# A two-layer transformer on one core: one transposing transfer per token tile, sums over later tokens in ScalarE's copy, elu's minimum on POOL, and a new timetable for layer 1

## The chip, the core and the metric

The kernel runs on one core of one Trainium2 chip. The metric is the device time of one execution in microseconds. The core's engines each run their own instruction stream in order and meet at semaphores: TensorE (PE; its weight loads are PEld), VectorE (DVE), ScalarE (ACT), GpSimd (POOL) and SyncE (SP), which here only issues transfers.

## What is computed

The input x is 16 batches of 512 tokens with 128 features, fp32. Cut to what matters here:

```python
xn = layernorm(x)
# layer 0: attention, 16 heads of 8, a bias within 64 tokens, causal
probs = softmax(q @ k.T * scale + bias)             # rope on q and k
out = relu(probs + tau / row) @ v                   # tau/row is added to masked tokens too
x = x + out @ Wo.T + fp4_ffn(xn)                    # weights, input and hidden go through fp4 blocks of 16
xn = layernorm(x)
# layer 1: linear attention, elu(.)+1 on q and k, running sums over tokens
kv, ks = cumsum(k x v), cumsum(k)
out = (q @ kv) / max(q . ks, 1e-6)
x = x + out @ w_out + moe(xn)                       # router over 4 experts, 2 chosen, and a shared expert
```

## The kernel before

A batch is four token tiles (T = 4) of 128 tokens. All work is laid out by hand on a grid of **slots**: a frame has 64 slots, and frame f computes in each slot s a piece of attention of batch f and, beside it, pieces of batches f-2 to f+1. A piece's place p counts from the start of its batch: p = 0 to 63 (the frame before the batch's attention) holds norm, projections, rope, the stacking of q and k and the fp4 gate; ATT + s lies beside its own attention; L1 + s is layer 1, one frame later; L1 + 64 and above reaches into the frame after that. Each engine walks over the same slots in the same order, so within an engine the order is fixed: first what belongs to the attention (scores, biased scores, exponentials), then the pieces of `EXTRAS` (which use the two PSUM banks of the scores), then the rest. The places stand in the table at lines 58 to 80.

**Attention of layer 0.** In each even slot TensorE makes two heads' scores (`scores`, L1122) into two banks that take turns; VectorE adds the bias and finds the maximum (`biased`, L584, `s_taken`); ScalarE takes the exponential with its sum (L954); VectorE inverts the four sums after every fourth slot (`row_rcp_of`, L591); POOL scales a slot later (`scale_probs`, L851); two to three slots on TensorE turns the blocks of 128 keys (`turn_probs`, L1132), ScalarE stores them with relu (`store_probs`, L963), and TensorE multiplies with v (`pv`, L1146).

**The turn banks.** Every transpose on TensorE takes a ticket q (`turn_ticket`, L1085) and bank 2 + q % 2, and waits until the bank's last content is stored (`t_taken`). ScalarE stores them in the order of the tickets. `intra` (L1247) also takes a turn ticket. In a slot with s % 4 == 0 up to two blocks are turned, in s % 4 == 2 the others. The `INTRA` pieces in even slots are made by TensorE ahead of the blocks, and stored by ScalarE at the slot's end (`beside`, L1019), which works as long as such a slot turns at most one block.

**Sums over later tokens.** A masked token still gets tau/row, so the output needs sums of v over the tokens of later tiles. TensorE takes the sums of xn over later tiles (`fx`, L1156, three matmuls of 3 columns, two fp32 passes each), VectorE copies them (`x_future`, L599), then `fv` (L1160) and `fy` (L1165) at slots 61 and 63 take them through Wv and Wo.

**Stacks.** q and k are split into fp16 high and low parts: ScalarE casts (L944, L945), POOL subtracts (L843, L844), and SyncE turns them by transposing transfers from `qx` and `kx` to `qkT0` (layer 0, two halves of the heads, 8 transfers of 256 columns each, in slot 33 and in the batch's own slot 1, `turn_stack0`, L410) and `qkT1` (layer 1, two transfers of 512 columns per tile in slots 28 to 31, `turn_stack1`, L422). `qkT0` has one buffer, so a half is turned when the earlier batch's scores of that half are done.

**Layer 1.** Projections in slots 20 to 23 (L1111), rope on VectorE (L557 to L564) and its addition on POOL (L836), elu: minimum on VectorE (`elu_low`, L647, three buffers), exponential on ScalarE (L981), maximum and sum on VectorE (`elu_high`, L651). Then `kv` (L1170), the turn of q (`q32`), the masked products `lin` (L1179 on TensorE, L616 on VectorE, pairs in odd slots from 35), `intra` (L1253), the totals `tot` (L1189, L1191). Between them the 15 gate and up matmuls of the experts (L1203, L1213; ScalarE's tanh L977, VectorE's L633 and L640), each expert's down matmuls in four quarters (`down1`, L1268), and VectorE's accumulation (`accumulate`, L708), four slots after an expert's first quarter. The router's 16 small VectorE steps stand two to a slot from slot 31 on, after a pair in slot 28.

Of the kernel before, what the change touches and what calls it, by code (L numbers as in the profile page):

```python
# [162 lines left out]
def build(nc, x, wq, wk, wv, wo, bias, tau, tau_col_in, wg, wu, wd, wqkv1, wout1, eg, eu, ed,  # L163
          cos, sin, ident, tri, inv_row, inv_col, head_mask, head_of, suffix, sel, lower, out):
# [3 lines left out]
    with ExitStack() as ctx:  # L168
# [230 lines left out]
        def _(sp):  # L399
# [10 lines left out]
            def turn_stack0(b, half):  # L410

                sp.wait_ge(lo_ok[0].sem, lo_ok[0].at(b, 2 * T))
                if has(b - 1):
                    sp.wait_ge(s_ps.sem, plan.score["score", b - 1, (half + 1) * SLOTS // 2 - 1] + 1)
                groups = slice(half * G // 2, (half + 1) * G // 2)
                heads = slice(half * H // 2, (half + 1) * H // 2)
                for t in range(T):
# [54 lines left out]
        def _(dve):  # L472
# [170 lines left out]
            def elu_low(b, t):  # L643
                dve.wait_ge(qk_ok[1].sem, qk_ok[1].at(b, t + 1))
                if t >= 3:
                    dve.wait_ge(elu_ok.sem, elu_ok.at(b, t - 2))
# [750 lines left out]
```

## Time and profile before

| | |
|---|---|
| runs | 2138.5, 2142.2, 2140.8 us; median 2140.8 |
| profiled execution | 2139.74 us, its span 2137.9 us |
| busy share of the span | TensorE 91%, VectorE 72%, ScalarE 64%, GpSimd 54% |
| TensorE weight loads | 59% |
| mean granted TensorE clock | 0.975 |
| chain that ended last | TensorE 53%, ScalarE 15%, VectorE 12%, POOL 7%, issue 7%, SyncE's queue 3% |

Busy shares are means over the whole span; the first frame and the last have less beside each other. In the timeline a row can hold several instructions (xN) and runs from the first one's start; a note in brackets is the engine's idle time ahead of it and what ended that. A wait is put down to the releaser that came last. Matmul ends are modelled, and a fp32 matmul is two passes, hence two instructions.

### The profile page before, as it was taken

The numbers are of one execution on the slowest core, as the hardware profiler recorded it, in microseconds if no ns is written. First come the engines' busy times: TensorE is split into PE (matmuls) and PEld (weight loads), VectorE is DVE, ScalarE is ACT, GpSimd is POOL, SyncE is SP. The second block draws the span as 40 slices with busy tenths as digits, with TensorE's granted clock in tenths as the row PEclk, the third lists the DMA queues.
The fourth block names the chain that finished last, engine by engine and source line by source line (L and its number), as shares of the span: only waits on it lengthen the run. The fifth ranks groups of instructions, "written<-read, shape, count | busy, mean of one in ns | idle before, by whom it ended". The sixth has DMA issues, their size and how long they took to land.

```text
span 2137.9 us, 50103 instructions
## 1 busy us (share of the span) xinstructions
PE 1939.8 (91%) x17353; PEld 1267.2 (59%) x17353; DVE 1544.0 (72%) x5224; ACT 1376.8 (64%) x3861; POOL 1148.3 (54%) x1800
## 2 busy tenths in 40 slices
PE   3788999999999998999999899999999999998968
PEld 1455665656566574656657566565656657565646
DVE  7557778687776868777686777868777676866745
ACT  1777585676857667585766758576685856757531
POOL 4685374745637465473746547374563746555220
PEclk7779999999999999999999999999999999999989
DMA  5011011110101111010111201111010111101010
GB/s 140 18 22 33 4 29 32 28 34 19 35 10 28 33 29 32 12 38 15 29 33 28 33 4 32 28 29 34 23 33 9 28 33 24 33 12 35 4 31 6
DMA packets 180848, 59.44 MB, mean 28 GB/s; under 512 B 147835, under 2 KB 178163, under 8 KB 180595
## 3 DMA queue, kind: packets, MB, share of 16 engines
q1 hardware_dynamic: 180595, 56.23, 12.3%
q8 instruction: 139, 2.28, 0.4%
q14 instruction: 114, 0.93, 0.1%
HBM read 14.22 MB, written 4.19 MB: 9 GB/s over the span
## 4 chain that ended last, share of the span: by engine, by line
PE 53%; ACT 15%; DVE 12%; POOL 7%; issue 7%; SPq 3%; DMA 2%; ACTq 0%; DVEq 0%; POOLq 0%
PE ps L1132 10%; PE ps L1268 8%; PE ps L1203 7%; PE ps L1213 6%; PE ps L1146 5%; ACT ring L954 5%; PE ps L1122 4%; ACT pb L963 3%; SPq L428 3%; PE ps L1253 3%; DVE ring L584 3%; PE ps L1191 2%; DVE lin L616 2%; PE ps L1111 2%; DMA qkT<-kx 2%
## 5 line engine op out<-in xcount | busy, mean ns | idle before, releaser
L851 POOL TENSOR_SCALAR ring<-ring,row_rcp,tau_row 128x128 f32<-128x128 f32 (+3 forms) x1024 | 629.6, 623 | 700.8 <-DVE row_rcp L591 700.8
L954 ACT ACTIVATE ring<-ring,neg_max 128x128 f32<-128x128 f32 (+3 forms) x1024 | 570.7, 558 | 504.0 <-DVE neg_max L584 499.5
L1132 PE MATMUL ps<-identf,ring 128*128 128x128 f32 x2560 | 378.7, 287 | 9.9 <-POOL ring L851 7.6
L963 ACT ACTIVATE pb<-ps 128x512 f32<-128x512 f32 x640 | 348.6, 584 | 29.6 <-PE ps L1132 25.5
L1132 PEld LDWEIGHTS ps<-identf,ring 128*128 128x128 f32 x2560 | 279.4, 143 | 83.2 <-issue 40.1
L584 DVE CUSTOM_DVE_ANT_1 ring<-ps,bias_t 128x384 f32<-128x384 f32 (+1 forms) x496 | 286.9, 614 | 55.0 <-PE ps L1122 47.8
L1268 PEld LDWEIGHTS ps<-ed_t,h 128*128 128x128 f32 (+1 forms) x1920 | 256.5, 192 | 98.3 <-issue 94.8
L1268 PE MATMUL ps<-ed_t,h 128*128 128x128 f32 (+1 forms) x1920 | 272.7, 278 | 0.0
L1203 PE MATMUL ps<-xn1T,eg_t 128*128 128x512 f32 (+1 forms) x480 | 256.6, 616 | 2.1 <-DVE h L633 2.1
L1213 PE MATMUL ps<-xn1T,eu_t 128*128 128x512 f32 (+1 forms) x480 | 256.6, 616 | 1.1 <-DVE h L640 0.9
L616 DVE TENSOR_TENSOR lin<-ps,tri_t 128x512 f32<-128x512 f32 x256 | 164.7, 685 | 127.8 <-PE ps L1179 127.8
L977 ACT ACTIVATE tanh_t<-ps 128x512 f32<-128x512 f32 (+2 forms) x304 | 172.0, 566 | 129.5 <-PE ps L1203 125.9
L1122 PE MATMUL ps<-qkT 32*128 32x128 f16 (+3 forms) x1024 | 200.5, 309 | 47.6 <-DVE neg_max L584 23.2
L1122 PEld LDWEIGHTS ps<-qkT 32*128 32x128 f16 x1024 | 62.1, 91 | 291.3 <-issue 110.6
L584 DVE CUSTOM_DVE_ANT_0 ring<-ps,bias_t 128x128 f32<-128x128 f32 (+1 forms) x528 | 171.8, 360 | 59.1 <-PE ps L1122 58.9
L1146 PE MATMUL ps<-pb,vx 128*32 128x128 f32 x5120 | 197.8, 281 | 1.8 <-ACT o_stack L969 1.6
L954 ACT ACTIVATION_READ_ACCUMULATOR ring<-ring,neg_max 128x1 f32 x1024 | 195.3, 191 | 0.0
L633 DVE SCALAR_TENSOR_TENSOR h<-tanh_t,ps 128x512 f32<-128x512 f32 (+1 forms) x240 | 163.2, 680 | 16.5 <-ACT tanh_t L977 16.4
L640 DVE SCALAR_TENSOR_TENSOR h<-h,ps 128x512 f32<-128x512 f32 (+1 forms) x240 | 163.1, 679 | 4.9 <-PE ps L1213 3.9
L1146 PEld LDWEIGHTS ps<-pb,vx 128*32 128x32 f32 x5120 | 125.9, 111 | 42.1 <-issue 24.6
L826 POOL TENSOR_TENSOR hid<-hid,q_step 128x352 f32<-128x352 f32 x128 | 100.8, 789 | 35.7 <-DVE q_step L725 35.7
L836 POOL TENSOR_TENSOR qk<-prod 128x256 f32<-128x256 f32 x128 | 92.7, 729 | 49.2 <-DVE prod L560 48.2
(154 smaller groups left out, 2822.0 us busy)
## 6 DMA issues: line engine op xcount, KB each, us to landing
x_t<-x SPq DMA_DIRECT2D x16, 256.0 KB, 3.1
x<-x SPq DMA_DIRECT2D x16, 256.0 KB, 2.9
o_rows<-o_stack SPq DMA_DIRECT2D x256, 16.0 KB
out<-x SPq DMA_DIRECT2D x16, 256.0 KB, 2.8
qkT<-qx SPq DMA_TRANSPOSE x192, 2.4
qkT<-kx SPq DMA_TRANSPOSE x192, 2.4
bias_t<-bias SPq DMA_DIRECT2D x1, 1536.0 KB, 8.0
eg_t<-eg SPq DMA_DIRECT2D x1, 860.0 KB
```

Of the source, the lines that this page charges most:

```text
L584: dve.tensor_tensor_reduce(out=dst, in0=src, in1=add, scale=-1.0, scalar=NO_MIN, op0=ALU.add, op1=ALU.min, accum_out=neg_max[:, n % 2, r:r ...
L616: dve.tensor_tensor(lin[:, k % NLIN, :, :], src.rearrange("p (t n) -> p t n", n=P), tri_t[:, :].unsqueeze(1).broadcast_to([P, T, P]), ALU. ...
L851: pool.tensor_scalar(e, e, row_rcp[:, m % 2, r:r + 1], tau_row[:, i, HG * g + r:HG * g + r + 1], ALU.mult, ALU.add).then_inc(p_ok.sem, 1)
L954: act.activation(e, e, ACT.Exp, bias=neg_max[:, n % 2, r:r + 1], scale=-1.0, accum_out=row_sum[:, n % 2, r:r + 1]).then_inc(exp_ok.sem, 1)
L963: act.activation(pb[:, c % NPB, :], bank(turn_bank(q)), ACT.Relu).then_inc(t_taken[q % 2].sem, 1)
L977: act.activation(tanh_t[0:rows, k % 2, 0:n], bank(G0)[0:rows, 0:n], ACT.Tanh, scale=0.5).then_inc(tanh_ok.sem, 1)
L1122: pe.matmul(o[:, 0:(i + 1) * P], qkT0[rows, g, 0, i * P:(i + 1) * P], qkT0[rows, g, 1, 0:(i + 1) * P], start=True, stop=True).then_inc(s_p ...
L1132: last = pe.transpose(o[:, r * P:(r + 1) * P], ring_of(i, r)[:, k * P:(k + 1) * P], idf)
L1146: last = pe.matmul(bank(PV)[R * r:R * (r + 1), i * P:(i + 1) * P], vx0[:, b % 2, k, v0:v0 + R], pb[:, c % NPB, r * P:(r + 1) * P], start=( ...
L1203: last = pe.matmul(bank(G0)[0:n, :], eg_t[:, e, r0:r0 + n], xn1T[:, :], start=True, stop=True)
L1213: last = pe.matmul(bank(G1)[0:n, :], eu_t[:, e, r0:r0 + n], xn1T[:, :], start=True, stop=True)
L1268: last = pe.matmul(o, h1[0:n, e % 2, c, ts], ed_t[0:n, e, c, :], start=(c == 0 and e < E), stop=(c == 2))
```

## The change

- `qx` and `kx` become one tensor `qkx`; each token tile is turned by one transfer of 1024 columns, four per batch and layer. `qkT0` has two buffers. Layer 0's transfers stand in slots 12 to 15, a slot after POOL's low parts; layer 1's stay in slots 28 to 31.
- `fx`, its constant and its VectorE copy go. ScalarE's copy of the turned x becomes a plain copy of tile 0 and three Identity activations whose sums give the tiles' column sums; POOL adds them up in slot 6 (`SUM_X`). `fv` and `fy` move from slots 61 and 63 to slots 1 and 3 of the next frame.
- elu's minimum moves from VectorE (slots 22 to 25) to POOL, right behind each tile's rope addition (slots 22 and 24), with four buffers.
- Layer 1's timetable: `kv` from slots 29, 29, 31 to 33, 47, 53; the turn of q from 30 to 46; the router from 31 to 37 (its last step in slot 43); `intra` from 40, 42, 46, 53 to 40, 44, 48, 52; down quarters of experts 1 and 2 from 42 and 48 to 44 and 49; accumulations of experts 0 to 2 from slots 39, 46, 52 to 43, 48, 53.
- ScalarE stores an `intra` of an even slot right behind that slot's first exponential, ahead of the blocks.

```diff
-TURN_X, FUTURE_X, QKV0, TURN_XQ = 5, 5, 7, 10
+TURN_X, QKV0, TURN_XQ = 5, 7, 10
...
-TURN_H, FUTURE_V, FUTURE_Y = (ATT + 11, ATT + 13, ATT + 13, ATT + 15), ATT + 61, ATT + 63
+TURN_H, FUTURE_V, FUTURE_Y = (ATT + 11, ATT + 13, ATT + 13, ATT + 15), ATT + 65, ATT + 67
...
-KV, TURN_Q32 = (L1 + 29, L1 + 29, L1 + 31), L1 + 30
+KV, TURN_Q32 = (L1 + 33, L1 + 47, L1 + 53), L1 + 46
...
-INTRA = (L1 + 40, L1 + 42, L1 + 46, L1 + 53)
+INTRA = (L1 + 40, L1 + 44, L1 + 48, L1 + 52)
...
-ROUTER = L1 + 31
+ROUTER = L1 + 37
...
-DOWN1 = [GATE1[3 * e + 2] + 4 for e in range(NE - 1)] + [L1 + 65]
+DOWN1 = [L1 + p for p in (35, 44, 49, 56, 65)]
+ADD_EXPERT = [L1 + p for p in (43, 48, 53, 60, 69)]
...
+SUM_X = TURN_X + 1
+TURN_STACK0, TURN_STACK1 = QKV0 + 5, QKV1 + 8
...
-        qx = [sb(f"qx{k}", [P, T, H, R], F16) for k in range(2)]
-        kx = [sb(f"kx{k}", [P, T, H, R], F16) for k in range(2)]
+        qkx = [sb(f"qkx{k}", [P, T, 2, H, R], F16) for k in range(2)]
...
-        qkT0 = sb("qkT0", [P, G, 2, L], F16)
-        qkT1 = sb("qkT1", [P, G, 2, L], F16)
+        qkT0 = sb("qkT0", [P, 2, 2, G, L], F16)
+        qkT1 = sb("qkT1", [P, 2, G, L], F16)
...
+            def turn_stack0(b, t):
+
+                sp.wait_ge(lo_ok[0].sem, lo_ok[0].at(b, 2 * t + 2))
+                if t == 0 and has(b - 2):
+                    sp.wait_ge(s_ps.sem, plan.score["score", b - 2, SLOTS - 1] + 1)
+                sp.dma_start_transpose(qkT0[:, b % 2, :, :, t * P:(t + 1) * P].rearrange("p a g n -> p (a g) n"),
+                                       qkx[0][:, t, :, :, :].rearrange("p a h r -> p (a h r)")).then_inc(st0_ok.sem, 16)
...
-                for a, v in enumerate((qx[1], kx[1])):
-                    sp.dma_start_transpose(qkT1[:, :, a, t * P:(t + 1) * P],
-                                           v[:, t, :, :].rearrange("p h r -> p (h r)")).then_inc(st1_ok.sem, 16)
+                sp.dma_start_transpose(qkT1[:, :, :, t * P:(t + 1) * P].rearrange("p a g n -> p (a g) n"),
+                                       qkx[1][:, t, :, :, :].rearrange("p a h r -> p (a h r)")).then_inc(st1_ok.sem, 16)
...
-                    if p in TURN_STACK0:
-                        turn_stack0(b, TURN_STACK0.index(p))
+                    if 0 <= p - TURN_STACK0 < T:
+                        turn_stack0(b, p - TURN_STACK0)
...
-                    if p == DOWN1[e] + 4:
+                    if p == ADD_EXPERT[e]:
                         accumulate(b, e)
...
+            def elu_low(b, t):
+                pool.wait_ge(qk_ok[1].sem, qk_ok[1].at(b, t + 1))
+                pool.tensor_scalar(elu_m[:, t, :], qk[:, t, :], 0.0, None, ALU.min).then_inc(elum_ok.sem, 1)
...
+                if p == SUM_X:
+                    v = x_future[:, b % 2, :]
+                    pool.wait_ge(t_taken[plan.turn["x", b, 0] % 2].sem, plan.turn["x", b, 0] // 2 + 1)
+                    pool.tensor_tensor(v[:, 1:2], v[:, 1:2], v[:, 2:3], ALU.add).then_inc(xs_ok.sem, 1)
+                    pool.wait_ge(xs_ok.sem, xs_ok.at(b, 1))
+                    pool.tensor_tensor(v[:, 0:1], v[:, 0:1], v[:, 1:2], ALU.add).then_inc(xs_ok.sem, T - 2)
...
                     if p == QKV1 + ROPE1[t] + 1:
                         rope_add(b, 1, t)
+                        elu_low(b, t)
...
-                    turned(("x", b, 0), xnT[:, :])
+                    q = plan.turn["x", b, 0]
+                    act.wait_ge(t_ps.sem, q + 1)
+                    if has(b - 2):
+                        act.wait_ge(s_ps.sem, plan.score["fv", b - 2, 0] + 1)
+                    act.copy(xnT[:, 0:P], bank(turn_bank(q))[:, 0:P])
+                    for t in range(1, T):
+                        ts = slice(t * P, (t + 1) * P)
+                        ins = act.activation(xnT[:, ts], bank(turn_bank(q))[:, ts], ACT.Identity, accum_out=x_future[:, b % 2, t - 1:t])
+                    ins.then_inc(t_taken[q % 2].sem, 1)
...
-                if p in INTRA:
-                    g = INTRA.index(p)
-                    turned(("intra", b, g), nd[:, g, :])
+                if p in INTRA and p % 2:
+                    store_intra(b, INTRA.index(p))
...
                 if has(f) and s % 2 == 0:
                     exp_with_sum(f, s)
+                for b, p in plan.beside(f, s):
+                    if p in INTRA and p % 2 == 0:
+                        store_intra(b, INTRA.index(p))
                 for blk in plan.blocks(f, s):
                     store_probs(*blk)
...
-                if s % (SLOTS // 2) == 0:
-                    pe.wait_ge(st0_ok[2 * s // SLOTS].sem, st0_ok[2 * s // SLOTS].at(b + 1, 0))
+                if s == 0:
+                    pe.wait_ge(st0_ok.sem, st0_ok.at(b + 1, 0))
...
-                if name == "fx":
-                    pe.wait_ge(xn_ok[0].sem, xn_ok[0].at(b, T))
+                if name == "fv":
                     o = score_ticket((name, b, k))
-                    for j in range(1, T):
-                        last = pe.matmul(o[:, 0:T - 1], xn[:, j, :], suffix_t[:, j, :], start=(j == 1), stop=(j == T - 1))
-                elif name == "fv":
-                    o = score_ticket((name, b, k))
-                    pe.wait_ge(s_taken.sem, plan.score["fx", b, 0] + 1)
+                    pe.wait_ge(xs_ok.sem, xs_ok.at(b, T - 1))
                     last = pe.matmul(o[:, 0:T - 1], wqkv0_t[:, 2 * D:3 * D], x_future[:, b % 2, :], start=True, stop=True)
```

## Rows read from the trace of the kernel before

**Rows 1.** Stretches: length, busy us (count) by engine, clock, DMA share, GB/s.

```profile
640.70:767.10 126.40, 119.15 (x1091) 78.40 (x1091) 95.30 (x327) 85.67 (x241) 71.34 (x112) 1.00 0.12 27
...
686.00:704.67 18.67, 16.20 (x118) 8.04 (x116) 17.30 (x66) 17.81 (x53) 12.36 (x24) 1.00 0.17 33
704.67:767.40 62.73, 60.91 (x597) 40.17 (x597) 48.61 (x146) 34.08 (x92) 23.35 (x36) 1.00 0.10 21
```

**Rows 2.** TensorE's waits, four frames from 893.6 us (total, times, longest).

```profile
PE ps L1179 <- DMA qkT<-kx: 6.6, 4, 1.8
...
PE ps L1165 <- DVE neg_max L584: 3.2, 4, 0.8
```

**Rows 3.** Timeline, slots 23 to 32: start, duration, engine, line, operation, wait.

```profile
689.14 0.29 DVE L647 TENSOR_SCALAR elu_m<-qk 128x256 f32<-128x256 f32 x1
...
691.57 0.56 POOL L851 TENSOR_SCALAR ring<-ring,row_rcp,tau_row 128x256 f32<-128x256 f32 x1 [1.82 <-DVE row_rcp L591]
...
698.01 0.72 ACT L954 ACTIVATE ring<-ring,neg_max 128x512 f32<-128x512 f32 x1
...
701.01 0.69 DVE L633 SCALAR_TENSOR_TENSOR h<-tanh_t,ps 128x512 f32<-128x512 f32 x1 [0.31 <-ACT tanh_t L977]
...
701.66 0.43 POOL L843 TENSOR_TENSOR qx<-qk,qx 128x128 f16<-128x128 f32 x1 [1.11 <-ACT kx L945]
...
702.46 0.48 PE L1170 MATMUL ps<-vx,qk 128*128 128x144 f32 x2 [1.32 <-DVE neg_max L584]
...
704.67 1.09 PE L1132 MATMUL ps<-identf,ring 128*128 128x128 f32 x8
```

**Rows 4.** Timeline, slots 63 to 6.

```profile
647.63 0.83 PE L1165 MATMUL ps<-wo_t,v_future 128*16 128x128 f32 x6 [0.79 <-DVE neg_max L584]
...
653.72 0.19 ACT L954 ACTIVATION_READ_ACCUMULATOR ring<-ring,neg_max 128x1 f32 x1
...
653.81 1.64 ACT L986 ACTIVATE xn<-x_t,shift,rstd 128x128 f32<-128x128 f32 x4
...
655.48 0.69 DVE L476 TENSOR_REDUCE x_step<-xn 128x32 f32<-128x512 f32 x1 [1.36 <-ACT xn L986]
...
657.32 0.80 PE L1156 MATMUL ps<-suffix_t,xn 128*128 128x3 f32 x6
...
658.43 0.63 PE L1099 MATMUL ps<-identf,xn 128*128 128x128 f32 x4 [0.31 <-ACT pb L963]
...
659.16 0.58 ACT L920 COPY xnT<-ps 128x512 f32<-128x512 f32 x1
```

**Rows 5.** Transposing transfers: lines 419 and 428, ns min/median/max.

```profile
L419 SPq DMA_TRANSPOSE qkT<-qx x128: 1167/1247/2427, 35.9 to 1922.6; - x128
...
DMA to landing us min/median/max: 2.3/2.4/4.8
...
L428 SPq DMA_TRANSPOSE qkT<-qx x64: 1188/1264/1998, 191.1 to 2078.2; - x64
...
DMA to landing us min/median/max: 2.4/2.5/5.0
```

**Rows 6.** Timeline, slots 39 to 44.

```profile
722.48 1.09 DVE L708 SCALAR_TENSOR_TENSOR x<-ps,comb,x 128x128 f32<-128x128 f32 x4
...
730.55 0.41 PE L1179 MATMUL ps<-qkT 32*128 32x128 f16 x8
...
733.03 0.69 DVE L584 CUSTOM_DVE_ANT_1 ring<-ps,bias_t 128x512 f32<-128x512 f32 x1
...
735.84 0.41 PE L1179 MATMUL ps<-qkT 32*128 32x128 f16 x8
```

**Rows 7.** Timeline, head and tail of the program.

```profile
47.47 0.29 PE L1122 MATMUL ps<-qkT 32*128 32x128 f16 x2 [7.79 <-DMA qkT<-kx]
...
53.05 0.28 DVE L584 CUSTOM_DVE_ANT_0 ring<-ps,bias_t 128x128 f32<-128x128 f32 x1
...
2082.07 0.62 PE L1179 MATMUL ps<-qkT 32*128 32x128 f16 x8 [4.96 <-DMA qkT<-kx]
```

More of the change, by code:

```diff
@@ L79 @@
          ("q32", (TURN_Q32,)), ("intra", INTRA), ("o1", (TURN_O1,)))
-EXTRAS = (("fx", (FUTURE_X,)), ("fv", (FUTURE_V,)), ("fy", (FUTURE_Y,)), ("kv", KV), ("lin", LIN), ("tot", TOT))
+EXTRAS = (("fv", (FUTURE_V,)), ("fy", (FUTURE_Y,)), ("kv", KV), ("lin", LIN), ("tot", TOT))
 def at(table, p):
@@ L163, in build @@
 def build(nc, x, wq, wk, wv, wo, bias, tau, tau_col_in, wg, wu, wd, wqkv1, wout1, eg, eu, ed,
-          cos, sin, ident, tri, inv_row, inv_col, head_mask, head_of, suffix, sel, lower, out):
+          cos, sin, ident, tri, inv_row, inv_col, head_mask, head_of, sel, lower, out):
     NB = x.shape[0]
@@ L244, in build @@
         nd = sb("nd", [P, G, L])
-        elu_m = sb("elu_m", [P, 3, 2 * D])
+        elu_m = sb("elu_m", [P, T, 2 * D])
         qT32 = sb("qT32", [P, L])
@@ L312, in build @@
         lo_ok = two("stack_low", 2 * T)
-        st0_ok = two("stack0_turned", 16 * 2 * T)
-        st1_ok = signal("stack1_turned", 16 * 2 * T)
+        st0_ok = signal("stack0_turned", 16 * T)
+        st1_ok = signal("stack1_turned", 16 * T)
         glog_ok = signal("router_logits_stored", T)
@@ L318, in build @@
         elu_ok = signal("elu_ready", T)
+        xs_ok = signal("x_future_ready", T - 1)
         s_ps = signal("scores_in_psum")
@@ L408, in store @@
                 sp.dma_start(out[bass.ds(b, 1)].rearrange("b (t p) d -> p (b t) d", p=P), x1[:, :, :]).then_inc(y_out.sem, 16)
[L410 to L417, printed above, removed]
-                    for a, v in enumerate((qx[0], kx[0])):
-                        sp.dma_start_transpose(qkT0[:, groups, a, t * P:(t + 1) * P],
-                                               v[:, t, heads, :].rearrange("p h r -> p (h r)")).then_inc(st0_ok[half].sem, 16)
+            def turn_stack0(b, t):
[4 more added lines that the diff above has]
+                                       qkx[0][:, t, :, :, :].rearrange("p a h r -> p (a h r)")).then_inc(st0_ok.sem, 16)
             def turn_stack1(b, t):
@@ L641, in hidden @@
                                          op0=ALU.mult, op1=ALU.mult).then_inc(g_taken[1].sem, 1)
[L643 to L646, printed above, removed]
-                dve.tensor_scalar(elu_m[:, t % 3, :], qk[:, t, :], 0.0, None, ALU.min).then_inc(elum_ok.sem, 1)
             def elu_high(b, t):
                 dve.wait_ge(elue_ok.sem, elue_ok.at(b, t + 1))
-                dve.scalar_tensor_tensor(out=qk[:, t, :], in0=qk[:, t, :], scalar=0.0, in1=elu_m[:, t % 3, :],
+                dve.scalar_tensor_tensor(out=qk[:, t, :], in0=qk[:, t, :], scalar=0.0, in1=elu_m[:, t, :],
                                          op0=ALU.max, op1=ALU.add).then_inc(elu_ok.sem, 1)
@@ L1178, in into_scores @@
                         ts = slice(t * P, (t + 1) * P)
-                        last = pe.matmul(o[:, ts], qkT1[rows, g, 1, ts], qkT1[rows, g, 0, ts], start=True, stop=True)
+                        last = pe.matmul(o[:, ts], qkT1[rows, 1, g, ts], qkT1[rows, 0, g, ts], start=True, stop=True)
                 else:
@@ L1349, in shape_constants @@
         head_mask[HD * h:HD * (h + 1), h, :] = 1
-    suffix = np.zeros((P, T, T - 1), f)
-    for j in range(T):
-        suffix[:, j, 0:j] = 1
     sel = np.zeros((P, HG, NV), f)
@@ L1362, in shape_constants @@
         "inv_row": np.broadcast_to(f(1) / (pos + 1), (P, L)), "inv_col": (f(1) / (pos + 1)).reshape(T, P).T,
-        "head_mask": head_mask, "head_of": head_of, "suffix": suffix, "sel": sel, "lower": lower,
+        "head_mask": head_mask, "head_of": head_of, "sel": sel, "lower": lower,
     }
```

34 lines of the change are left out of this document (14 added, 20 removed).

## The prediction, made before the change was run

> **What bounds the kernel now.** The first view is the page's busy times by engine: TensorE works 91% of the span, VectorE 72%, ScalarE 64%, GpSimd 54%. The second is the table of stretches. A frame (64 slots; batch f's attention beside layer 1 of f-1 and the projections of f+1) lasts 126.4 us, TensorE is busy for 119 of them [rows 1], and fifteen frames, f = 1 to 15, hold layer 1 beside attention. Third, the list of waits says where the missing 7 us go: over four frames 6.6 us for the transposing transfers ahead of the first `lin` and 3.2 us at `fy` [rows 2]; the timeline adds 1.32 us a frame at the third `kv` [rows 3]. The timeline of one frame also tells which stretch is bound by what. From slot 36 to the frame's end TensorE hardly waits: what is put there is paid for. In slots 20 to 32 it waits for a chain over the other engines [rows 1, 3]: ScalarE is busy 17.8 of 18.7 us. The same edit therefore has a different price in each stretch.
>
> **What the change does to a steady frame, stretch by stretch.** Times are those of the frame that starts near 641 us. X is the start of slot 43's `lin` on TensorE.
>
> *Slots 61 to 6.* `fy` leaves slot 63, where it waited 0.79 us for the scores' bank and took 0.8; `fv` (0.24) leaves slot 61. They come back in slots 1 and 3. FX (six passes, 0.80 us) goes. But slot 5 is not held by FX: the turn of x waited until 658.43 for ScalarE's store of a probability block, which was late because VectorE's slot 4 stood behind the quantiser's reduction, which waited for ScalarE's norm [rows 4]. Replaying this chain without `fv` and `fy` in slots 61 to 63 (VectorE 0.2 us earlier, row reciprocals 0.2, POOL's rstd and the norm 0.7) brings the turn of x to about 657.65, 0.8 us earlier. Then ScalarE's copy of 0.58 us [rows 4] becomes one copy of 128 columns and three Identity passes with a sum. No row has that form. The norm's four passes of 128 columns take 1.64, and a read of the accumulator is 0.19 by itself [rows 4]. From below: the four passes with a cheaper first one, 1.3; from above: 1.64 and three reads, 2.2. I take 1.5, near the norm's passes, whose shape is the same and beside which a read can run. That is 0.9 more, and the second block of slot 6 needs this bank: it starts at 660.05 instead of 659.79. Net **+0.3 us** (-0.8 if the copy's length did not count, +0.9 at the upper end). POOL's two sums of one column (0.2 us each) wait in slot 6 behind the same copy and push the quantiser's addition by 0.3 us; its result has 2 us to spare.
>
> *Slots 20 to 32.* POOL takes four minima. VectorE's cost 0.29 each; POOL's nearest row is its scaling of 256 columns, 0.56 [rows 3]; bounds 0.29 and 0.8. Two of them delay the scaling of slots 25 to 27 by 1.1 us, so the blocks of slot 28 start some 0.3 us later, although the scores ahead of them come 0.85 us earlier (VectorE freed). Both `kv` groups of slot 29, the turn of q and the `kv` of slot 31 go. TensorE then waits for what it does not make itself: the gate of slot 31 needs slot 28's silu (701.01 + 0.6), and slot 32's blocks need POOL's fourth scaling, which stands behind the low halves of tile 2, which stand behind ScalarE's casts at 701.5; ScalarE runs almost without a gap (17.8 of 18.7 us, rows 1) up to and behind the exponential at 698.01 [rows 3]. None of these is lightened but by 0.15 us. So slot 32's transposes still start at about 704.5: **-0.15 us**, and the wait at `kv` comes back as two others.
>
> *Slot 35.* Eight transposing transfers of 1.26 us are issued one after another; the last lands 2.5 us after its issue, which is when `lin` starts [rows 5]. The waits give 6.6/4 = 1.65 us a frame. After the change four are issued, the last after POOL's last low half (about 703.9), and land by 707.2, ahead of TensorE's 709.2: **-1.65 us**. From 256 to 512 columns a transfer's issue grew from 1.247 to 1.264 us and its landing from 2.4 to 2.5 [rows 5]; now it has 1024. I take 1.3 and 2.8. The upper bound is proportional, 2.53 us each, the same ten microseconds in all: then nothing is gained here. The Trainium skill speaks for that bound: its page DMA: Bandwidth & Descriptors (section Why a DMA increments its semaphore by 16 and not by 1) has a transpose inside SBUF, on the generations before the newest, pay one push command for every tile; by that the four would take as long as the eight, and the sum would be 30 us more. The rows of 256 and 512 columns do not agree with a price per tile.
>
> *Work that moves into the full stretch.* Three `kv` at 0.3 us and the turn of q at 0.6 now stand in slots 33, 46, 47 and 53: **+1.5 us**.
>
> *Slots 42 to 45.* This is the large term. Before, `intra` 1 was in slot 42, experts' down quarters in 42 to 45, the first accumulation in slot 39 (1.09 us of VectorE) [rows 6]. Now slot 42 loses 1.0 + 0.77 us of TensorE work but its gate waits 0.5 for slot 40's silu, so X is 728.98 (before 730.55). VectorE: end of `hidden` 729.6, two `lin` 1.29, silu 0.6, reciprocal, two router steps 0.4, accumulation 1.1 and its wait 0.26; only then slot 44's biased scores, 733.3 to 733.9. ScalarE takes slot 44's exponential (0.7) first and then `intra` 1's copy (0.58): done at 735.35. Slot 44 now asks for three turn tickets (`intra`, block 0, block 1) with two banks, so block 1 waits for that copy; TensorE is there at 733.0. A wait of 2.35 us. Behind it queue gate 44, a down quarter and `lin` 45, which starts at 737.5 instead of 735.84, with two down quarters (2 x 0.77) still to be done: +3.2, and I take **+3.1 us**. The lower bound, only VectorE's work of before ahead of the scores (X + 2.5, rows 6), leaves 1.1 us of the wait; the upper one is the 2.35 of the order as written.
>
> *Slots 48 and 52* get the same three tickets with nothing heavy ahead of the exponential: 0.2 us each, **+0.4 us**. The second and third accumulations (slots 48, 53) find slack.
>
> **Sum.** 0.3 - 0.15 - 1.65 + 1.5 + 3.1 + 0.4 = +3.5 us a frame, times 15 = +52. The tail (batch 15 alone): the wait of 4.96 us for the transfers [rows 7] goes, 1.5 us of moved work and 0.6 at the accumulation come: -2.6. The head: TensorE waits 7.8 us for transfers at 47.47, but VectorE takes up the first scores only at 53.05, busy until then with the quantiser [rows 7]: transfers that land earlier gain 0 (if VectorE were done earlier it would be up to 5.5 us, once). The execution took 2139.7 us (span 2137.9): 2139.7 + 52 - 2.6 = 2189, and with the 1.1 us by which the median of the runs lies above this execution, 2190.
>
> **The rivals.**
> *No wait at slot 44.* If the copy of `intra` 1 is there in time (the scores of slot 44 not behind the accumulation), 2.35 us a frame fall away: 2190 - 35 = 2155. For it: TensorE reached slot 44 of the frame before without a wait. Against: both orders are written down and are kept in order.
> *The chain of slots 20 to 32 shortens.* This is the one on the other side. VectorE loses four minima, router steps and masks here. If ScalarE's work starts as much earlier as TensorE loses work and waits (1.5 + 0.85 + 1.3 = 3.65 us instead of 0.15), the frame comes to 0.0; together with only the lower 1.1 us of the wait in slot 44 it is -1.25 us, thus -19 - 2.6: 2119. It decides from the point where slot 32's transposes start before about 701. For it: TensorE's waits there are among the largest of the frame [rows 3]. Against: ScalarE is busy for 17.8 of these 18.7 us [rows 1], so that a freed VectorE has hardly a gap to close.
> *Transfers no cheaper.* The proportional bound: +1.65 us a frame and nothing won in the tail, 2190 + 25 + 5 = 2220. For it only the page; against it the two widths in the rows.
> *Nearly nothing* (the moved waits balance): 2141.
>
> **Chances.** Forecast 0.50; no wait at slot 44 0.14; transfers no cheaper 0.05; shorter chain 0.25; nearly nothing 0.06. A measurement of this kernel can tell a difference of about 0.2%, 4 us, from none. Faster 0.26, same 0.05, slower 0.69. The slower cases alone reach from 2148 (2155 less 0.5 us a frame) to 2206 (2190 plus 0.6 at the copy and 0.5 in slots 48 and 52). The range of 8 in 10 takes in most of the shorter chain: 2115 to 2206, leaving out its lowest part and the transfers' case.
>
> **What would show it.** In the changed profile: TensorE idle at the transposes of blocks behind ScalarE's store of `nd`, once a frame by about 2 us and twice by 0.2; waits for `qkT` gone; at slots 31 and 32 waits of TensorE for silu and for POOL's scaling, together near 2 to 3 us; ScalarE's busy time up by about 0.9 us a frame; frames of about 130 us. I would be wrong if the frames are at or under 126.4 us, if no block waits for `nd`, or if slots 20 to 32 take under 16 us.

## The result, and the profile after

The changed kernel takes 2198.8 us (median of 4 runs, 2197.6 to 2200.8) against 2141.5 us (4 runs, 2138.5 to 2142.9): ratio 1.027, 95% interval 1.0253 to 1.0288. The profiled execution took 2197.9 us, its span is 2196.1 us, 58.2 us more than before. The forecast was 2190 us.

The page of the changed kernel: TensorE's busy share fell from 91% to 89%, and in the chain that ended last POOL has 10% instead of 7%.

```profile
PE 1955.8 (89%) x17257; PEld 1258.7 (57%) x17257; DVE 1505.6 (69%) x5143; ACT 1386.3 (63%) x3957; POOL 1207.3 (55%) x1895
...
PE 53%; DVE 14%; ACT 14%; POOL 10%; issue 8%; DMA 0%; SPq 0%; DVEq 0%; ACTq 0%; POOLq 0%
```

The stretches of a steady frame, batch 5's (its first score starts at 660.02), as [rows 1] of before: the frame is 130.17 us long instead of 126.40, with the same TensorE work (118.8 us busy, before 119.2). Slots 20 to 32 (second line) last 18.3 us instead of 18.7, with 2.0 us less of TensorE work in them; what is longer is the rest (third line), 66.45 instead of 62.73 us.

```profile
651.74:781.91 130.17, 118.81 (x1081) 77.25 (x1080) 92.56 (x321) 86.28 (x249) 75.07 (x119) 1.00 0.13 26
698.75:717.04 18.29, 14.19 (x108) 6.79 (x106) 14.46 (x55) 17.45 (x52) 15.73 (x28) 1.00 0.26 44
717.04:783.49 66.45, 62.56 (x602) 40.87 (x603) 47.88 (x149) 34.81 (x93) 23.30 (x36) 1.00 0.04 8
```

TensorE's waits over the whole run. The transfers, 1.65 us a frame in the four frames of [rows 2] (1.45 in the mean of frames 1 to 14, between 0.92 and 2.35), hold `lin` once, in the tail. In their place stand POOL's scaling (L839), waited for at the blocks' transposes (L1140), and ScalarE's store of `nd` (L915), once in each of 15 frames.

```profile
PE ps L1140 <- POOL ring L839: 48.6, 56, 2.2
PE ps L1140 <- ACT nd L915: 34.2, 15, 2.3
PE ps L1130 <- DVE neg_max L579: 26.6, 51, 10.6
PE ps L1206 <- DVE h L626: 13.9, 27, 1.3
...
PE ps L1182 <- DMA qkT<-qkx: 1.8, 1, 1.8
```

Where they are, in the timeline of that frame (TensorE alone; before in [rows 3] and [rows 6]): blocks of slot 28, gate of slot 31, blocks of slot 32; then the gate of slot 42, and the blocks of slot 44 (block 0, then block 1 behind its wait), of slot 48 and of slot 52.

```profile
710.16 1.09 PE L1140 MATMUL ps<-identf,ring 128*128 128x128 f32 x8 [2.21 <-POOL ring L839]
...
714.20 1.09 PE L1206 MATMUL ps<-xn1T,eg_t 128*88 128x512 f32 x2 [0.91 <-DVE h L626]
...
717.04 1.09 PE L1140 MATMUL ps<-identf,ring 128*128 128x128 f32 x8 [0.82 <-POOL ring L839]
...
739.53 1.13 PE L1206 MATMUL ps<-xn1T,eg_t 128*128 128x512 f32 x2 [0.26 <-DVE h L626]
...
744.41 0.66 PE L1140 MATMUL ps<-identf,ring 128*128 128x128 f32 x4
747.35 0.66 PE L1140 MATMUL ps<-identf,ring 128*128 128x128 f32 x4 [2.29 <-ACT nd L915]
...
756.45 1.43 PE L1140 MATMUL ps<-identf,ring 128*128 128x128 f32 x8
...
766.66 1.43 PE L1140 MATMUL ps<-identf,ring 128*128 128x128 f32 x8
```

Eight such transposes take 1.09 us where nothing holds them up. In slot 44 they take 3.60 us from first start to last end, 2.51 more, and in slots 48 and 52 they take 0.34 us more each: 3.2 us a frame at the three places with a third ticket.

The chain behind the last one, over VectorE and ScalarE: the last router step and the accumulation run up to the biased scores of slot 44, ScalarE waits 3.95 us for these and takes the exponential and only then `nd`.

```profile
743.58 0.20 DVE L682 TENSOR_TENSOR comb<-gs,gsum 128x16 f32<-128x16 f32 x1
743.90 1.13 DVE L695 SCALAR_TENSOR_TENSOR x<-ps,comb,x 128x128 f32<-128x128 f32 x4
745.28 0.69 DVE L579 CUSTOM_DVE_ANT_1 ring<-ps,bias_t 128x512 f32<-128x512 f32 x1 [0.25 <-PE ps L1140]
...
746.01 0.72 ACT L949 ACTIVATE ring<-ring,neg_max 128x512 f32<-128x512 f32 x1 [3.95 <-DVE neg_max L579]
...
746.73 0.56 ACT L915 COPY nd<-ps 128x512 f32<-128x512 f32 x1
```

The prices that no row of before had. Grouped by line: POOL's minimum, the copy of tile 0, and the two transposing transfers (issue; then issue to landing).

```profile
L824 POOL TENSOR_SCALAR elu_m<-qk x64: 843/847/897, 179.0 to 2129.0; 128x256 f32<-128x256 f32 x64
...
L995 ACT COPY xnT<-ps x16: 240/258/266, 12.3 to 1846.6; 128x128 f32<-128x128 f32 x16
...
L416 SPq DMA_TRANSPOSE qkT<-qkx x64: 1231/1238/2483, 31.8 to 1865.2; - x64
...
DMA to landing us min/median/max: 3.0/3.2/4.8
```

### The profile page after: what moved, and what is told of

Read it like the earlier page. It is cut to its first block, busy times and chain, and to the rows that moved or that the text cites. A ratio compares the mean times of both kernels' runs of the same rounds, so it can differ in the third digit from the quotient of the medians.

```text
span 2196.1 us, 49715 instructions
## 1 busy us (share of the span) xinstructions
PE 1955.8 (89%) x17257; PEld 1258.7 (57%) x17257; DVE 1505.6 (69%) x5143; ACT 1386.3 (63%) x3957; POOL 1207.3 (55%) x1895
## 4 chain that ended last, share of the span: by engine, by line
PE 53%; DVE 14%; ACT 14%; POOL 10%; issue 8%; DMA 0%; SPq 0%; DVEq 0%; ACTq 0%; POOLq 0%
PE ps L1140 10%; PE ps L1271 8%; PE ps L1206 8%; PE ps L1216 6%; PE ps L1154 5%; ACT ring L949 4%; PE ps L1130 4%; DVE lin L609 3%; POOL ring L839 3%; DVE ring L579 3%; PE ps L1194 3%; ACT pb L958 2%; PE ps L1256 2%; PE ps L1182 2%; POOL qk L820 2%
## 5 line engine op out<-in xcount | busy, mean ns | idle before, releaser
L839 POOL TENSOR_SCALAR ring<-ring,row_rcp,tau_row 128x128 f32<-128x128 f32 (+3 forms) x1024 | 629.5, 622 | 739.5 <-DVE row_rcp L586 739.5
L1140 PE MATMUL ps<-identf,ring 128*128 128x128 f32 x2560 | 389.9, 287 | 95.2 <-POOL ring L839 48.6
L1140 PEld LDWEIGHTS ps<-identf,ring 128*128 128x128 f32 x2560 | 277.6, 143 | 183.3 <-POOL ring L839 77.2
L958 ACT ACTIVATE pb<-ps 128x512 f32<-128x512 f32 x640 | 354.3, 586 | 26.2 <-PE ps L1140 26.1
L1216 PE MATMUL ps<-xn1T,eu_t 128*128 128x512 f32 (+1 forms) x480 | 265.1, 635 | 3.6 <-DVE h L633 3.6
L1130 PE MATMUL ps<-qkT 32*128 32x128 f16 (+3 forms) x1024 | 208.7, 310 | 44.2 <-DVE neg_max L579 26.6
```

What stands on the lines that cost most here:

```text
L839: pool.tensor_scalar(e, e, row_rcp[:, m % 2, r:r + 1], tau_row[:, i, HG * g + r:HG * g + r + 1], ALU.mult, ALU.add).then_inc(p_ok.sem, 1)
L958: act.activation(pb[:, c % NPB, :], bank(turn_bank(q)), ACT.Relu).then_inc(t_taken[q % 2].sem, 1)
L1130: pe.matmul(o[:, 0:(i + 1) * P], qkT0[rows, b % 2, 0, g, i * P:(i + 1) * P], qkT0[rows, b % 2, 1, g, 0:(i + 1) * P], start=True, stop=True ...
L1140: last = pe.transpose(o[:, r * P:(r + 1) * P], ring_of(i, r)[:, k * P:(k + 1) * P], idf)
L1216: last = pe.matmul(bank(G1)[0:n, :], eu_t[:, e, r0:r0 + n], xn1T[:, :], start=True, stop=True)
```

## The experiments

A frame's length is taken as the distance from its first score to the next frame's, the mean over frames 1 to 14: before 126.97, after 130.83 us. Differences between slots inside a frame are taken between the medians of these frames unless the mean is named; where the clock changes in some frames only, the two differ. The times of the kernel before, measured beside the experiments, were 2139.9, 2140.4 and 2139.2 us (medians of 8, 13 and 11 runs).

**1. The whole old timetable.** `KV`, `TURN_Q32`, `INTRA`, `ROUTER`, `DOWN1` and `ADD_EXPERT` as before, the rest as changed.

```diff
-KV, TURN_Q32 = (L1 + 33, L1 + 47, L1 + 53), L1 + 46
-INTRA = (L1 + 40, L1 + 44, L1 + 48, L1 + 52)
-ROUTER = L1 + 37
-DOWN1 = [L1 + p for p in (35, 44, 49, 56, 65)]
-ADD_EXPERT = [L1 + p for p in (43, 48, 53, 60, 69)]
+KV, TURN_Q32 = (L1 + 29, L1 + 29, L1 + 31), L1 + 30
+INTRA = (L1 + 40, L1 + 42, L1 + 46, L1 + 53)
+ROUTER = L1 + 31
+DOWN1 = [L1 + p for p in (35, 42, 48, 56, 65)]
+ADD_EXPERT = [L1 + p for p in (39, 46, 52, 60, 69)]
```

> The changed kernel with all of layer 1's places as before (kv, turn of q, intra, router, down quarters, accumulations); transfers, sums in ScalarE's copy, minima on POOL, fv and fy stay as changed. My theory (the timetable is what costs, the rest gives): a steady frame is 126.45 of before, +0.3 for slots 61 to 6, -0.15 and -1.65 for slots 20 to 36, nothing else, so 125.0 us instead of 130.2; 15 frames give -22 and the tail -5: about 2114 us, ratio to the kernel before 0.987. No block waits for nd. Rival (POOL's minima are the main cost, since waits for its scaling grew from 0.5 to 3.2 us a frame): only the 2.3 us a frame of the nd wait goes, about 2160 us, ratio 1.009.

Measured: 2124.7 us, ratio 0.9932 (0.9915 to 0.9948), frames 126.08 us. The timetable is the cost, and nothing is left of the wait for `nd`; but 10 us of what I expected are missing. TensorE's timeline and the windows (their third column from the right is the granted clock) say why: the wait for POOL in slot 28 stayed, and behind it the clock was 0.70 and 0.73, a mix of its two levels (1.2 and 2.4 GHz). That it costs time shows between the frames of this one execution: slots 20 to 36 last 26.7 us in the only one of the 14 frames in which the clock stayed at 1.00 there (that frame lasts 124.7 us, the expected 125.0), and 28.0 (their median) in the 13 others.

```profile
692.50 1.36 PE L1140 MATMUL ps<-identf,ring 128*128 128x128 f32 x8 [2.22 <-POOL ring L839]
```

```profile
682.00:692.00 10.00, 8.13 (x70) 3.95 (x69) 8.93 (x35) 9.34 (x31) 8.79 (x13) 1.00 0.03 6
692.00:695.00 3.00, 2.50 (x10) 1.83 (x11) 2.10 (x9) 3.00 (x8) 3.00 (x7) 0.70 0.23 44
695.00:698.00 3.00, 3.00 (x11) 1.64 (x10) 1.63 (x4) 2.21 (x8) 1.65 (x4) 0.73 0.76 140
```

**2. Only the places of `intra`.**

```diff
-INTRA = (L1 + 40, L1 + 44, L1 + 48, L1 + 52)
+INTRA = (L1 + 40, L1 + 42, L1 + 46, L1 + 53)
```

> The changed kernel with only the intra pieces in slots 40, 42, 46, 53 again. My theory (block 1 of slots 44, 48 and 52 waits for ScalarE's store of nd, a third ticket on two banks): the wait of 2.29 us in slot 44 and two shorter ones go, 2.7 us a frame, about 2159 us; frames of 127.5 us. Rival (VectorE's order ahead of slot 44 is the bound, and the wait only moves to the scores of slot 46 or to the gate): under 0.7 us a frame, 2190 us or more, with a new wait of TensorE in slots 44 to 47.

Measured: 2146.6 us, ratio 1.0039 (1.0025 to 1.0053): 52 us gone of 58. No block waits for `nd`; in the mean slot 46 comes 2.4 us earlier after the frame's start, slot 54 2.8. Slots 36 to 62 last 3.7 us less in the mean, where I had expected 2.7: the blocks of slots 44, 48 and 52 were held up by 3.2 us and not by the 2.5 us of their waits, and 0.4 is the clock, which fell to 0.88 in slots 44 to 48 in 4 of 14 frames of the changed kernel, each 1.6 us longer, and here in none. VectorE's order does not take the wait's place: the gate waits 0.2 us.

**3. elu's minimum on VectorE** (with the new timetable): `elu_low` stands in VectorE's slots 22 to 25 again, and no longer behind POOL's rope addition.

```diff
+                if 0 <= p - QKV1 - 2 < T:
+                    elu_low(b, p - QKV1 - 2)
...
                         rope_add(b, 1, t)
-                        elu_low(b, t)
```

> The changed kernel with elu's minimum on VectorE in slots 22 to 25 again. My theory (slots 20 to 32 are bound by the chain over ScalarE, POOL's scaling and VectorE's products whoever takes the minima): TensorE's wait of 2.2 us at slot 28's blocks gets smaller, but slot 36 starts within 0.3 us of where it did, 2199 us within 5. Rival (POOL's four minima hold up its scaling and with it the frame): slots 28 to 36 shorten by 1 to 2.2 us, 2168 to 2184 us.

Measured: 2226.3 us, ratio 1.0401 (1.0378 to 1.0424): 27 us slower, outside both expectations. The wait in slot 28 goes, and one of 2.67 us for silu comes at the gate of slot 31 (the second half of my theory). Slot 36 starts 0.9 us later than in the changed kernel, slot 46 2.3 us (in the mean 1.1 and 1.8, and 15 times 1.8 is 27). The wait for `nd` is as long as before (2.29), so it isn't that; behind it the clock was down, which it was not in the same frame of the changed kernel. Windows of slots 44 to 46:

```profile
750.00:754.00 4.00, 1.99 (x45) 1.45 (x44) 3.60 (x13) 1.06 (x3) 2.59 (x4) 1.00 0.02 4
754.00:757.00 3.00, 2.72 (x11) 1.94 (x12) 0.12 (x1) 2.55 (x6) 0.00 (x0) 0.71 0.00 0
757.00:760.00 3.00, 3.00 (x21) 1.72 (x19) 1.88 (x3) 0.00 (x0) 0.00 (x0) 0.72 0.00 0
```

**4. Only `kv` and the turn of q.**

```diff
-KV, TURN_Q32 = (L1 + 33, L1 + 47, L1 + 53), L1 + 46
+KV, TURN_Q32 = (L1 + 29, L1 + 29, L1 + 31), L1 + 30
```

> The changed kernel with kv in slots 29, 29, 31 and the turn of q in slot 30 again. My theory (there TensorE waits anyway, 3.9 us of waits in slots 28 to 32, and from slot 33 on every piece is paid for): 1.5 us a frame come back, frames of 128.7 us, about 2176 us. Rival (the pieces need the score banks and a turn bank, so they lengthen slots 28 to 32 by what they take off later): 2199 us within 5.

Measured: 2183.3 us, ratio 1.0211 (1.0186 to 1.0235): 15.5 us instead of 22.5. From slot 44 on the frame gains 1.38 us, so the moved work cost its full price there. But slot 36 starts 0.92 us later, and the clock was below 1.00 in slots 28 to 36 in 13 of 14 frames, against 7 in the changed kernel. The same wait of 2.22 us stands ahead of it in both. In the one frame at full clock slots 20 to 36 last 26.7 us, no more than in the changed kernel, and in twelve of the others 27.8 (table below). One window at a lower clock:

```profile
709.00:712.00 3.00, 2.40 (x9) 2.10 (x10) 1.76 (x7) 2.71 (x8) 3.00 (x7) 0.53 0.21 43
```

So three runs had met the same thing, and the next four took the parts one by one from the side of the kernel before.

**5. Transfers and sums.** Run 1 and run 3 together: only the transfers, ScalarE's sums with `fv` and `fy` in slots 1 and 3, and the order of the `intra` stores stay.

> The run with the old timetable, and elu's minimum on VectorE too: what stays of the change is one transfer per tile, the sums in ScalarE's copy with fv and fy in slots 1 and 3, and ScalarE's order of the intra stores. My theory (the 2.2 us wait for POOL's scaling in slot 28 comes from POOL's minima, and it also brings stretches of a lower granted clock in slots 28 to 31): that wait goes, the clock stays at 1.00 there, slots 20 to 36 last 1.8 us less than in the kernel before, frames 125.0 us, about 2112 us, 12 us under the run with the minima on POOL. Rival (as with the new timetable, where VectorE's minima made the kernel 27 us slower): 2130 to 2150 us, with a wait for VectorE's silu at the gate of slot 31.

**6. Transfers only.** The kernel before with `qkx`, one transfer per tile, two buffers of `qkT0`, four of `elu_m`, and the order of the `intra` stores.

```diff
-TURN_STACK0, TURN_STACK1 = (33, ATT + 1), QKV1 + 8
+TURN_STACK0, TURN_STACK1 = QKV0 + 5, QKV1 + 8
```

> The kernel before with one transposing transfer per tile and two buffers of qkT0, and ScalarE's intra store ahead of the blocks; sums, minima and timetable as before. My theory: the wait for the transfers at slot 35 goes (1.65 us a frame) and the tail's wait falls from 5.0 to some 2 us, nothing else moves: frames 124.8 us, 2141 - 25 - 3 = about 2113 us. Rival (transfer time proportional to width or the gain lost in the next wait): 2135 us or more.

Measured: run 5 2121.0 us, 0.9912 (0.9897 to 0.9927); run 6 2109.9 us, 0.9862 (0.9846 to 0.9879), the fastest kernel of this study. Run 6 is near the first expectation of 2113: slots 20 to 36 last 1.66 us less than before (1.46 in the mean, as much as the waits for the transfers that are gone). Slots 40 to 44 last 0.24 us less too, in every frame: the wait of 0.17 us for `nd` in slot 43 is gone with the order of the `intra` stores (runs 7 and 8 keep the old order and the wait), so some 4 of the 30 us are not the transfers'. Run 5 had to be 4.5 us above it (0.3 us a frame) and is 11. From slot 28 on the two kernels do the same work with the same wait of 1.60 us at the `kv` of slot 31, and differ in the clock. The same frame (the seventh), run 5 first, then run 6:

```profile
943.00:946.00 3.00, 1.93 (x10) 0.73 (x14) 2.93 (x12) 2.97 (x10) 2.72 (x6) 0.83 0.66 129
946.00:949.00 3.00, 3.00 (x26) 2.31 (x27) 1.97 (x8) 1.70 (x5) 3.00 (x5) 0.60 0.67 127
```

```profile
944.00:947.00 3.00, 1.58 (x10) 0.75 (x14) 2.97 (x9) 2.96 (x10) 2.38 (x6) 1.00 0.58 110
947.00:950.00 3.00, 2.92 (x28) 1.76 (x28) 2.67 (x12) 2.64 (x8) 3.00 (x5) 1.00 1.22 115
```

**7. The minima on POOL only**, in the kernel before (with four buffers).

```diff
-                if 0 <= p - QKV1 - 2 < T:
-                    elu_low(b, p - QKV1 - 2)
...
                         rope_add(b, 1, t)
+                        elu_low(b, t)
```

> The kernel before with only elu's minimum moved to POOL. My theory (POOL's minima, 4 of about 0.5 us, hold up the scaling that slot 28's blocks need, TensorE waits there, and the granted clock falls in the stretch behind): a wait of about 2 us at slot 28's blocks for POOL, 0.3 to 1.3 us a frame more by slot 36, 2145 to 2160 us. Rival (the minima on POOL free VectorE, which is what slots 28 to 32 wait for): faster by 0.5 us a frame or more, 2133 us or less.

Measured: 2136.5 us (10 runs), 0.9982 (0.9972 to 0.9991), frames 126.48 us: neither. The wait of 2.2 us for POOL at slot 28 is there, as is the lower clock (in 14 of 14 frames), yet slot 36 starts 0.3 us earlier in the mean than in the kernel before: what slots 28 to 32 lose, the transfers have caught up, and their wait of 0.9 us at `lin` is gone. In the kernel before the minima on POOL hide behind the transfers; with the transfers cheap they don't (run 1 against run 5: 4 us).

```profile
947.77 1.39 PE L1129 MATMUL ps<-identf,ring 128*128 128x128 f32 x8 [2.21 <-POOL ring L847]
```

**8. The sums only**, in the kernel before (`fx` and its copy gone, `fv` and `fy` in slots 1 and 3).

```diff
-TURN_H, FUTURE_V, FUTURE_Y = (ATT + 11, ATT + 13, ATT + 13, ATT + 15), ATT + 61, ATT + 63
+TURN_H, FUTURE_V, FUTURE_Y = (ATT + 11, ATT + 13, ATT + 13, ATT + 15), ATT + 65, ATT + 67
+SUM_X = TURN_X + 1
```

> The kernel before with only the sums of later tokens from ScalarE's copy, and fv and fy in slots 1 and 3. My theory: slots 61 to 6 last 0.3 us more in each steady frame, as in the changed kernel, 15 frames 4.5 us, and frame 15 loses 1.2 us where fv and fy leave it: 2143 to 2146 us. Rival (six matmul passes fewer and VectorE's copy gone are worth something): 2136 us or less.

Measured: 2148.6 us, 1.0045 (1.003 to 1.006), 2.6 us above the range that I expected. Slots 61 to 8 cost the 0.3 us a frame; another 0.5 in the mean come in slots 34 and 35, where the wait for the transfers grew from 1.45 to 1.73 us. The sums are a loss by themselves.

**9. `intra` and minima**: runs 2 and 3 together.

> The changed kernel with intra in slots 40, 42, 46, 53 and elu's minimum on VectorE, both together. With VectorE's minima alone the frame grew by 0.9 us up to slot 36 and by 1.4 us in slots 44 to 46, where the granted clock was about 0.7 behind the wait for nd. My theory (the 1.4 us are the clock behind a wait of 2.3 us; without the wait they don't come): 10 to 14 us over the run with intra's places alone (2146.6), 2156 to 2161 us, clock 1.00 in slots 44 to 46. Rival (VectorE's minima cost 27 us by themselves): 2174 us.

Measured: 2158.6 us, 1.0094 (1.0081 to 1.0107). 12 us over run 2, and the clock was 1.00 in slots 44 to 48 in all 14 frames:

```profile
990.30:997.00 6.70, 6.33 (x45) 3.77 (x44) 5.69 (x16) 3.03 (x8) 2.59 (x4) 1.00 0.00 0
```

The other 15 of run 3's 27 us don't come without the wait for `nd`, but not all of them lie behind it: against the changed kernel, run 3 loses 0.7 us a frame in slots 44 to 48, where its clock was down in 10 frames instead of 4, some 10 us in all. The rest comes in slots 24 to 36, where run 2, which run 9 is measured against, already had a lower clock in 11 frames and the changed kernel in 7.

**10. Router and accumulation.** With `intra` in its new places.

```diff
-ROUTER = L1 + 37
-ADD_EXPERT = [L1 + p for p in (43, 48, 53, 60, 69)]
+ROUTER = L1 + 31
+ADD_EXPERT = [L1 + p for p in (39, 48, 53, 60, 69)]
```

> The changed kernel with the router from slot 31 and expert 0's accumulation in slot 39 again, intra still in 40, 44, 48, 52. My theory (VectorE's router steps and accumulation ahead of slot 44's biased scores make up about half of the wait for nd): the wait of 2.29 us falls to about 1.1 us, frames of 129.0 us, about 2181 us. First rival (what holds the store of nd is ScalarE's exponential for another reason): wait and time stay, 2199 us within 4. Second rival (the router's steps back in slots 31 to 36 lengthen the chain there as much): 2190 us or more with a smaller wait for nd.

Measured: 2170.9 us, 1.0161 (1.0139 to 1.0182), 28 us under the changed kernel. The wait for `nd` did not halve, it went (2.3 us in the whole run instead of 34.2); half a microsecond of it came back at the gate of slot 42, which now waits 0.81 us for silu. The third tickets are still there (slot 44's transposes take 1.44 us, as in slots 48 and 52), so the long wait needs both: the third ticket, and a store of `nd` that is late behind VectorE's router steps and accumulation. Taking away either ends it. The waits of the whole run:

```profile
PE ps L1206 <- DVE h L626: 16.9, 21, 1.9
...
PE ps L1140 <- ACT nd L915: 2.3, 6, 0.4
```

This kernel also shows the clock in its time: its profiled execution took 2181.8 us at a mean granted clock of 0.958, its three other runs 2169.5 to 2171.4 at 0.972 to 0.973. The mean clock alone doesn't give the time, though: the ten runs of experiment 7 have clocks from 0.967 to 0.978, and at 0.967 it took 2137.2 us, at 0.978 2135.8.

**11 and 12. Two tries to better run 6:** the router from slot 33 instead of 31, and the minima split (tiles 0 and 1 on POOL, 2 and 3 on VectorE).

```diff
-ROUTER = L1 + 31
+ROUTER = L1 + 33
```

> The run with the transfers only (2109.9 us), and the router from slot 33 instead of 31. Theory A (VectorE is a link of the chain that slots 28 to 32 wait for, TensorE waits 1.6 us for its neg_max at slot 31's kv): four steps of 0.2 us leave slots 31 and 32, up to 0.5 us a frame, about 2103 us. Theory B (the chain goes over ScalarE and POOL, as the prediction had it): 2110 us within 3.

```diff
+                if T // 2 <= p - QKV1 - 2 < T:
+                    elu_low(b, p - QKV1 - 2)
...
+                        if t < T // 2:
+                            elu_low(b, t)
```

> The run with the transfers only (2109.9 us), and elu's minimum of tiles 0 and 1 on POOL, of tiles 2 and 3 on VectorE. Theory A (either engine with all four minima is late for something in slots 28 to 31; split, neither is): no wait over 1.2 us in slots 28 to 31, up to 0.5 us a frame less, 2102 to 2106 us. Theory B (ScalarE's chain bounds the stretch whatever the others do): 2110 us within 3. Theory C (POOL's scaling is late with two minima too and the clock falls behind the wait): over 2113 us.

Measured: 2127.9 us (6 runs, 0.9949, 0.9934 to 0.9963) and 2112.0 us (0.9874, 0.986 to 0.9889). The first is 18 us above run 6 and outside both theories: in slots 30 to 34 0.7 us a frame in the mean (1.36 between the medians), where the clock was down in 9 of 14 frames instead of 3 (below), and 0.4 in slots 40 to 44, where the gate of slot 42 now waits 0.33 us for silu. The wait at the third `kv` was no shorter (1.69). The second came out as theory B has it: the wait there stays 1.55 us with two minima on either engine. It ends with VectorE's biased scores, and VectorE in turn had waited for ScalarE's tanh just ahead of them (third line below, run 12; the first two are run 11's windows), 0.81 us in run 6.

```profile
950.00:953.00 3.00, 2.10 (x4) 0.82 (x4) 2.93 (x10) 2.62 (x8) 2.88 (x6) 0.67 0.70 132
953.00:956.00 3.00, 3.00 (x29) 1.95 (x29) 1.33 (x7) 1.90 (x6) 2.67 (x4) 0.77 0.64 121
...
694.86 0.69 DVE L627 SCALAR_TENSOR_TENSOR h<-tanh_t,ps 128x512 f32<-128x512 f32 x1 [0.77 <-ACT tanh_t L974]
```

The clock of all kernels, over slots 28 to 36 of frames 1 to 14 of the one profiled execution of each, which for run 10 is its slowest ("lost": the stretch's time times one minus its clock, mean of a frame; the last column is the median length of slots 20 to 36 in the frames at full clock and in those with a clock near 0.90). In the kernel before and in run 8 that length also varies with the wait for the transfers. Slots 44 to 48 had a clock under 1.00 in 4 frames of the changed kernel, 10 of run 3, 1 of run 4, 9 of run 10, and in none of the others.

| kernel | longest wait there, median of the frames, us | frames with clock under 1.00 | lost, us | slots 20 to 36, us |
|---|---|---|---|---|
| before | 1.5 | 4 | 0.29 | 28.1 / 29.3 |
| after | 2.2 | 7 | 0.85 | 26.9 / 27.0 |
| 1, old timetable | 2.2 | 13 | 1.58 | 26.7 / 28.0 |
| 2, intra | 2.2 | 11 | 1.58 | 26.9 / 27.5 |
| 3, minima on VectorE | 2.7 | 13 | 1.95 | 27.1 / 27.7 |
| 4, kv and q | 2.2 | 13 | 1.71 | 26.7 / 27.8 |
| 5, transfers and sums | 1.6 | 7 | 0.85 | 26.9 / 28.3 |
| 6, transfers | 1.6 | 3 | 0.37 | 26.9 / 28.2 |
| 7, minima on POOL | 2.2 | 14 | 1.71 | - / 28.1 |
| 8, sums | 1.8 | 5 | 0.38 | 28.8 / 30.1 |
| 9, intra and minima | 2.7 | 10 | 1.71 | 27.1 / 27.8 |
| 10, router and add | 2.2 | 14 | 2.44 | - / 26.9 |
| 11, router from 33 | 1.7 | 9 | 1.10 | 27.2 / 28.3 |
| 12, minima split | 1.6 | 4 | 0.49 | 26.7 / 28.0 |

So "lost" is not time added. In the changed kernel a lower clock in slots 28 to 36 costs 0.1 us a frame, because other waits take it up: the gate of slot 28 takes 1.88 us instead of 1.02, and the waits at slots 31 and 32 (0.91 and 0.82 us in batch 5's frame) are gone. The first row is batch 5's frame at full clock, the second that of batch 7 at the lower one:

```profile
711.09 1.02 PE L1206 MATMUL ps<-xn1T,eg_t 128*128 128x512 f32 x2
...
971.41 1.88 PE L1206 MATMUL ps<-xn1T,eg_t 128*128 128x512 f32 x2
```

Where `kv` and the turn of q fill these holes (runs 1, 4, 5, 6, 11 and 12), the lower clock costs 1.1 to 1.3 us a frame.

## Why the prediction was right

The sign, the mechanism and the place of the largest term held. By its own steps:

- **Slots 61 to 6, +0.3: measured +0.30** (in the frame of batch 5: slots 60 to 64 last 1.42 us less, slots 0 to 8 1.71 more), by two errors that cancel. ScalarE's copy takes 1.04 us, not 1.5, and lies under my lower bound of 1.3: each read of a sum runs beside the next pass, four passes start 0.25 us apart. But the turn of x came 0.16 us earlier, not 0.8; my replay of the chain ahead of it was too hopeful.
- **Slots 20 to 32, -0.15: measured -0.37** for slot 32's transposes. Inside the stretch a term was mis-sized: a minimum on POOL takes 0.85 us, above both the 0.56 that I took and the upper bound of 0.8, and slot 28's blocks start 1.25 us later instead of 0.3. The waits of TensorE add up to 3.9 us instead of 2 to 3. That the stretch's end hardly moves is what the step said; run 12, with the minima split, agrees with it. The Trainium skill (GPSIMD Engine Reference, section 4.1 Engine selection) calls POOL with one input roughly line-rate. Against that, 0.85 us here stand beside VectorE's 0.29 [rows 3]: this case does not agree.
- **Slot 35, -1.65: right.** From slot 20 to 36 the frame lasts 1.69 us less (forecast -1.5 with the `kv` of slot 33). The four frames behind the term had longer waits than the rest, 1.65 us for 1.45 in the mean of all. The issue of a transfer took 1.24 us at 1024 columns, as at 256 and 512 [rows 5], the landing 3.2 us (I took 2.8). Run 6 shows it nearly alone. The Trainium skill (DMA: Bandwidth & Descriptors, Why a DMA increments its semaphore by 16 and not by 1) gives one push command per tile for this transfer on the generations before the newest; an issue time that stays the same from 256 to 1024 columns does not agree with it.
- **Moved work +1.5, slots 42 to 45 +3.1, slots 48 and 52 +0.4: right.** Slots 42 to 62 last 4.88 us more (forecast 4.7); the wait is 2.29 us for 2.35 and holds the blocks up by 2.51, and the two small ones by 0.34 each instead of 0.2. What the prediction gave as its lower bound, 1.1 us of wait without the accumulation in the way, was wrong: run 10 took router and accumulation out and the wait was gone, but for 0.34 us.
- **The sum.** The frame of the first table lasts 130.17 us, +3.8 for +3.5; the mean over 14 frames is +3.86. Of that, 0.44 are the four frames with a lower clock in slots 44 to 48 (1.56 us each); the lower clock in slots 28 to 36 of 7 frames adds under 0.1. Over the whole span: the head -3.05 (I had 0: VectorE did take up the first scores at the same time, but `fv` and `fy` are gone from the first frame too, and run 8, with the sums alone, has the same 3.2), 14 frames +54.0, the last frame with the tail +7.2 instead of +0.9 (the tail's terms as the prediction lists them add to -2.9, not -2.6). Of the last, 4.4 us are the clock in slots 12 to 36 of batch 15's frame, where the kernel before ran at 1.00:

```profile
1979.92:1998.24 18.32, 14.12 (x133) 10.24 (x126) 7.87 (x37) 13.75 (x39) 9.01 (x14) 0.91 0.08 20
1998.24:2020.20 21.96, 19.49 (x123) 10.58 (x123) 13.38 (x49) 17.43 (x51) 15.64 (x28) 0.77 0.15 28
```

- **The rivals.** "No wait at slot 44", "transfers no cheaper" and "nearly nothing" are refuted by the rows above. "The chain of slots 20 to 32 shortens" had 0.25 and was worth 0.2 us a frame; runs 7 and 12 show that it is not worth more. What no case of mine had is that the clock falls behind the longer waits: 6.2 us in slots 44 to 48 and 4.4 in the last frame, more than the whole 8.8 us by which the forecast was low. That the head gave back 3.05 of it was luck.

Left open: why the clock fell in 7 frames of run 5 and in 3 of run 6 behind the same wait of 1.60 us. The runs show that it did, not what decided.

## What to carry to other kernels

Count the holders of a shared buffer in each slot before moving a piece there. Undoing the third tickets on two banks gave back 52 of the 58 us here, and undoing what made their store late gave back 28, so the two don't add up. Such a ticket shows only as a wait for a store that stands behind other pieces in another engine's fixed order. Take the parts of a change apart: this one held a gain of 30 us (one transfer per tile and the order of the `nd` stores) under a loss of 89. And put movable work where TensorE waits anyway, but read the granted clock of that stretch as well. Behind a hole of 1.5 us or more a lower clock cost over 1 us where the stretch was full, and next to nothing where further waits took it up.
